# A fused cross-attention and gated feed-forward kernel: K and V of the first group fetched during the K stage, a query unit in two pieces, the last quad in another order

## The reference, cut to what matters

```python
def _L0_xattn_ref(latents, context, Wq, Wk, Wv, Wo):      # latents: layernorm(x); b=8, q_len=128, HIDDEN=512
    hidden_states = jnp.concatenate([context, latents], axis=1)          # 256 keys
    q = (latents @ Wq).reshape(b, q_len, N_KV_HEADS, N_GROUPS, HEAD_DIM) # 4 x 8 heads of 128
    k = (hidden_states @ Wk).reshape(b, kv_len, N_KV_HEADS, HEAD_DIM)
    v = (hidden_states @ Wv).reshape(b, kv_len, N_KV_HEADS, HEAD_DIM)
    scores = jnp.einsum('bqhgd,bkhd->bhgqk', q, k) * scale
    attn = jax.nn.softmax(scores.astype(jnp.float32), axis=-1).astype(q.dtype)
    out = jnp.einsum('bhgqk,bkhd->bqhgd', attn, v)
    return out.reshape(b, q_len, N_HEADS * HEAD_DIM) @ Wo
def _L0_ffn_ref(x, weight, bias, gate_w, in_channel_scale, out_channel_scale):
    routing = jax.nn.softmax((xf @ gate_w.T).astype(jnp.float32), axis=1)   # 8 experts
    in_scale = routing @ in_channel_scale
    out_scale = routing @ out_channel_scale
    wb = ste_sign(weight)                                                   # signs of 512 x 512
    return (xf * in_scale @ wb.T * out_scale + bias)
x = x + _L0_xattn_ref(_layernorm(x), ctx_4096, Wq, Wk, Wv, Wo)
x = x + _L0_ffn_ref(_layernorm(x), weight, bias, gate_w, in_channel_scale, out_channel_scale)
```

## Time and profile before

| what | us |
|---|---|
| median of 3 runs | 686.14 (684.45 to 686.57) |
| the profiled execution | 686.85 |
| its span, first to last instruction | 685.1 |
| outside the span | 1.75 |
| PE busy | 669.3 |
| DVE, ACT, POOL busy | 449.0, 354.3, 301.6 |

### The profile page before, as it was taken

How to read it: one execution, slowest core, us unless ns; L and a number is a source line. 1 busy time by engine, 2 the same in 40 slices (tenths; PEclk the granted TensorE clock), 3 DMA queues, 4 the chain that set the end, 5 groups by cost and what they waited for, 6 DMA issues and landing times.

```text
span 685.1 us, 10290 instructions
## 1 busy us (share of the span) xinstructions
PE 669.3 (98%) x3376; PEld 564.0 (82%) x3376; DVE 449.0 (66%) x752; ACT 354.3 (52%) x881; POOL 301.6 (44%) x248
## 2 busy tenths in 40 slices
PE   7999999999999999999999999999999999989997
PEld 4888887878888888888888888888888888868875
DVE  5653233666767776776677776767767776768766
ACT  3344322744565456545654565556455544566643
POOL 4135000542374337324632463246334638755674
PEclk9999999999999999999999999999999999999999
DMA  9556547688658876766698867667977565645511
GB/s 325 221 206 239 205 203 249 194 262 268 185 190 253 277 244 221 215 186 194 197 279 258 250 190 217 192 191 204 277 271 250 184 203 189 193 152 155 158 42 67
DMA packets 90836, 144.84 MB, mean 211 GB/s; under 512 B 15208, under 2 KB 48232, under 8 KB 89760
## 3 DMA queue, kind: packets, MB, share of 16 engines
q1 hardware_dynamic: 90784, 144.19, 66.1%
HBM read 91.60 MB, written 52.56 MB: 210 GB/s over the span
## 4 chain that ended last, share of the span: by engine, by line
PE 89%; DMA 4%; DVE 3%; ACT 2%; issue 1%; SPq 1%; POOL 0%; ACTq 0%; DVEq 0%
PE bank L1102 48%; PE bank L1216 24%; PE bank L1201 12%; DMA p_park<-p_turned 2%; PE bank L1292 2%; DMA kg<-k_park 1%; DVE bank L920 1%; DMA raw_a<-in_L_xattn_Wv 1%; ACT prob L633 1%; PE bank L1111 1%; PE bank L1243 0%; PE bank L1266 0%; PE bank L1119 0%; POOL p_low L462 0%; ACT wq_pair L550 0%
## 5 line engine op out<-in xcount | busy, mean ns | idle before, releaser
L462 POOL TENSOR_TENSOR p_low<-p_low,p_high 128x1024 fp32r<-128x1024 f32 x64 | 153.6, 2400 | 268.0 <-ACT p_high L550 267.9
L1216 PE MATMUL bank<-wo_pair,oT 128*128 128x512 f32 x768 | 188.3, 392 | 1.5 <-DVE oT L812 1.5
L1102 PE MATMUL bank<-xT,wq_pair 128*128 128x512 f32 x768 | 185.4, 391 | 0.0
L1216 PEld LDWEIGHTS bank<-wo_pair,oT 128*128 128x128 f32 x768 | 139.9, 188 | 28.4 <-issue 2.1
L1102 PEld LDWEIGHTS bank<-xT,wq_pair 128*128 128x128 f32 x768 | 140.5, 188 | 26.7
L633 ACT ACTIVATE prob<-bank,nmax 128x256 f32<-128x256 f32 x256 | 118.9, 470 | 34.3 <-DVE nmax L890 34.2
L550 ACT ACTIVATE oT<-bank 128x512 fp32r<-128x512 f32 x64 | 38.4, 600 | 185.7 <-DVE bank L920 185.5
L905 DVE STREAM_TRANSPOSE p_turned<-prob 128x512 f32<-128x512 f32 x128 | 91.1, 711 | 57.1 <-ACT prob L633 57.1
L1102 PEld LDWEIGHTS bank<-kg,qT 128*128 128x128 f32 x768 | 107.6, 190 | 12.0 <-DMA kg<-k_park 1.9
L1102 PE MATMUL bank<-kg,qT 128*128 128x256 f32 x768 | 111.5, 283 | 2.0 <-DMA kg<-k_park 1.5
L890 DVE TENSOR_REDUCE nmax<-bank 128x2 f32<-128x512 f32 x128 | 87.6, 686 | 37.8 <-PE bank L1102 37.8
(11 more groups left out here) (92 smaller groups left out, 602.3 us busy)
## 6 DMA issues: line engine op xcount, KB each, us to landing
p_park<-p_turned SPq DMA_DIRECT2D x64, 512.0 KB, 4.1
p_low<-p_park SPq DMA_DIRECT2D x64, 512.0 KB, 4.6
r_all<-r_park SPq DMA_DIRECT2D x64, 256.0 KB, 4.4
v_park<-v_stage SPq DMA_DIRECT2D x8, 1024.0 KB, 4.3
raw_a<-in_L_xattn_Wq SPq DMA_DIRECT2D x32, 256.0 KB, 5.2
raw_b<-in_L_xattn_Wo SPq DMA_DIRECT2D x32, 256.0 KB, 4.9
k_park<-k_stage SPq DMA_DIRECT2D x8, 1024.0 KB, 3.8
kg<-k_park SPq DMA_DIRECT2D x32, 256.0 KB, 5.4
```

The lines of the kernel that those rows point to most:

```text
L462: nc.gpsimd.tensor_tensor(part, part.bitcast(fp32), p_high[:, :].rearrange("p i c q -> p (i c q)"), ALU.subtract).then_inc(p_lo, 1)
L1102: last = nc.tensor.matmul(dst, left(a, c), right(b, c), start=(n == 0), stop=(n == 3 * chunks - 1))
L1216: last = nc.tensor.matmul(wo_bank[:, :], oT[:, s, h, :], wo_pair[:, w, h, :], start=((s, w) == TERMS[0] and h == 0), stop=((s, w) == TERMS ...
```

## The change

It does six things. (1) SP loads `kg` and `vg` of the first group in the K stage, right behind the parks of units 2 to 5, four batches at a time; the tiles are laid out anew so that they lie on `wv_pair` and `craw`, which are free by then. (2) At the start, the transposes of the first x come after the whole first product; the second product waits for the high part of x alone at first; DVE makes all four low parts of Wv before the first `layer_norm`, and the second batch's statistics after it. (3) The fourth query unit (u = 3 of the first quad) is made in two pieces, the 128 columns of batch 0 first. (4) In the last quad, ACT's `p_half(t + 1)` comes before `exps(t + 3, 0)`, and in step 1 DVE's statistics of batch 0 come after `o_scale(1)`. (5) In steps 5 and 6 the HI part of `ffn_product(t - 3)` comes before `logits(t - 2)`, and in step 7 there is none: `ffn_product(4)` and its `ffn_scale` are in the tail. (6) In the tail the products, logits and routes stand in another order, and product 5 has a bank of its own.

```diff
@@ -298,6 +302,20 @@
+                if u == 2:
+                    sp.wait_ge(proj_ready, 2 * B)
+                    sp.wait_ge(ct_ready, B)
+                    for i in range(2):
+                        sp.wait_ge(v_parked[i], 16 * (B // 2))
+                if 2 <= u < 2 + NHALF:
...
+                    for b in range(half * HALF, (half + 1) * HALF):
+                        load_k(0, b)
+                elif 4 <= u < 6:
+                    for b in range((u - 4) * HALF, (u - 3) * HALF):
+                        load_v(0, b)
@@ -618,8 +627,14 @@
+                done = 0
+                if first and u == QH - 1:
+                    done = T
+                    nc.scalar.activation(qT[:, HI, h, 0:T], proj_bank[u % 2][:, 0:T], ACT.Copy,
+                                         scale=SCALE).then_inc(first_hi, 1)
+                    act.wait_ge(first_lo, 1)
+                nc.scalar.activation(qT[:, HI, h, half * 512 + done:(half + 1) * 512],
@@ -838,13 +853,12 @@
             for c in range(HC):
-                if c == 2:
-                    dve.wait_ge(x_in[1], 16)
-                    layer_stats(1, 1)
-                    layer_norm(0, 0)
...
+            layer_norm(0, 0)
+            dve.wait_ge(x_in[1], 16)
+            layer_stats(1, 1)
             xt_rest(0)
@@ -1017,8 +1038,11 @@
-                ffn_stats(t - 1)
+                if t > 1:
+                    ffn_stats(t - 1)
                 o_scale(g, qd, t)
+                if t == 1:
+                    ffn_stats(t - 1)
@@ -1136,9 +1161,11 @@
-                            {1: lambda: pe.wait_ge(ct_lo, 1), 2: lambda: xt_transpose(0)}
-                            if n == 0 else {}
+                            {0: {1: lambda: pe.wait_ge(ct_lo, 1)},
+                             1: {1: lambda: pe.wait_ge(xt_lo, 1)}}.get(n, {})
                             ).then_inc(proj_ready, 1)
+                    if n == 0:
+                        xt_transpose(0)
@@ -1174,7 +1201,10 @@
+                if g == 0 and qd == 0 and t == 0 and p == 1:
+                    pe.wait_ge(proj_lo, PRE_UNITS + QH - 1)
+                    pe.wait_ge(first_lo, 1)
@@ -1325,6 +1357,8 @@
                 attend(g, qd, t)
+                if LEAD <= t < B - 1 and t + LEAD >= B:
+                    ffn_product(t - 3, (HI,))
                 if t >= 2:
                     logits(t - 2)
@@ -1333,8 +1367,8 @@
-                if t >= 3:
-                    ffn_product(t - 3)
+                if LEAD <= t < B - 1:
+                    ffn_product(t - 3, (HI, LO) if t + LEAD < B else (LO,))
@@ -1365,14 +1399,15 @@
             logits(B - 2)
-            ffn_product(B - 3, (HI,))
+            ffn_product(B - 4)
             y_transpose(B - 1)
             route_transpose(B - 2)
+            ffn_product(B - 3, (HI,))
+            logits(B - 1)
+            channel_scales(B - 2)
             ffn_product(B - 3, (LO,))
-            channel_scales(B - 2)
-            logits(B - 1)
+            route_transpose(B - 1)
             ffn_product(B - 2, (HI,))
-            route_transpose(B - 1)
             channel_scales(B - 1)
```

More of the change, by code:

```diff
@@ L335, in fetch_r @@
                              ).then_inc(r_in[t % 2], 16)
[L337 to L340, removed]
             park_p(0, 0, 0)
@@ L620, in q_half @@
                     act.wait_ge(s_ready[h // 2], steps(g, qd, HALF * (half + 1) - B))
-                nc.scalar.activation(qT[:, HI, h, half * 512:(half + 1) * 512],
-                                     proj_bank[u % 2][:, :], ACT.Copy, scale=SCALE
+                done = 0
[5 more added lines that the diff above has]
+                nc.scalar.activation(qT[:, HI, h, half * 512 + done:(half + 1) * 512],
+                                     proj_bank[u % 2][:, done:512], ACT.Copy, scale=SCALE
                                      ).then_inc(proj_hi, 1)
@@ L754, in final_step @@
                     gate_exp(t - 2)
+                if t + 1 < B:
+                    p_half(g, qd, t + 1)
                 if t + LEAD < B:
@@ L876, in _, with q_rest @@
                              k_stage[:, u % 2, :, HI, :, kc, :]).then_inc(proj_lo, 1)
-            def q_rest(g, qd, u):
+            def q_rest(g, qd, u, first=False):
                 half, h = divmod(u, QH)
+                done = 0
+                if first and u == QH - 1:
+                    done = T
+                    dve.wait_ge(first_hi, 1)
+                    nc.vector.scalar_tensor_tensor(qT[:, LO, h, 0:T], proj_bank[u % 2][:, 0:T], SCALE,
+                                                   qT[:, HI, h, 0:T], ALU.mult, ALU.subtract
+                                                   ).then_inc(first_lo, 1)
                 dve.wait_ge(proj_hi, count(g, UNITS, qd, PRE_UNITS + u + 1))
-                cols = slice(half * 512, (half + 1) * 512)
-                nc.vector.scalar_tensor_tensor(qT[:, LO, h, cols], proj_bank[u % 2][:, :], SCALE,
+                cols = slice(half * 512 + done, (half + 1) * 512)
+                nc.vector.scalar_tensor_tensor(qT[:, LO, h, cols], proj_bank[u % 2][:, done:512], SCALE,
                                                qT[:, HI, h, cols], ALU.mult, ALU.subtract
@@ L1035, in final_step @@
                     gate_factor(t - 2)
[L1036 removed]
+                if 3 <= t < B - 1:
                     ffn_scale(t - 3)
@@ L1052, in _ @@
             for u in range(QH):
-                q_rest(0, 0, u)
+                q_rest(0, 0, u, first=True)
             for t in range(LEAD):
@@ L1071, in _ @@
             gate_route(B - 2)
+            ffn_scale(B - 4)
             gate_factor(B - 2)
-            ffn_scale(B - 3)
-            z_make(B - 2)
-            gate_max(B - 1)
-            z_rest(B - 2)
-            gate_route(B - 1)
-            gate_factor(B - 1)
+            gate_max(B - 1)
+            z_make(B - 2)
+            gate_route(B - 1)
+            z_rest(B - 2)
+            gate_factor(B - 1)
+            ffn_scale(B - 3)
             z_make(B - 1)
@@ L1285, in ffn_product @@
                             pe.wait_ge(sgnt_copied, HC)
-                        elif b < B - 2:
+                        elif b < B - 3:
                             pe.wait_ge(scaled_ready, b)
+                        elif b == B - 3:
+                            pe.wait_ge(acc_ready, steps(G - 1, QUADS - 1, B))
                         else:
```

29 lines of the change are left out of this document (12 added, 17 removed).

## The result

The changed kernel takes 696.04 us (median of 4 runs, 694.54 to 696.66) beside 685.89 for the kernel before in the same runs: a ratio of 1.0135, 95% interval 1.0117 to 1.0152. By the ratio it is 9.3 us slower (by the medians 10.15), where 684.8 was predicted and the range ended at 687.2. Its profiled execution takes 695.43 us and has a span of 693.6, 8.5 longer than the 685.1 before.

What follows compares the result with a forecast made beforehand. PE, busy 669.3 of 685.1 us, was taken as the bound. Terms 0.3 - 1.5 - 0.2 - 0.1 + 1.7 - 0.3 - 1.5 = -1.6 gave 685.25 from 686.85; it said 684.8, range 682.5 to 687.2.

Steps and rivals of the forecast that it cites:

- steps 1 to 4: Last quad: later statistics lose time, earlier `p_half` wins it back; together -0.1 us (-0.5 to +0.5).
- the tail: Step 7 to the last product: -0.3 us without product 4 before the projection, then -1.5 (+0.2 to -2.0).
- Steps 5 and 6: Last quad: HI parts ahead of the logits make each LO part wait longer, +0.85 us per step, +1.7 in all.
- statistics +1.2: Step 1 of the last quad: statistics after `o_scale(1)` delay `o_half(1)` and PE's projection by 1.2 us.
- `p_half` -1.5: Step 2 of the last quad: POOL finishes before `attend(2)`, so the 1.2 us wait and a smaller one go.
- "just late": Steps 5 and 6: `z_half` arrives slightly late for the HI part, adding 0.15 us before the logits end.
- the order's terms: Tail: product 4 adds 1.84 us, vanishing waits give -2.3, a new wait for the last z adds 0.65.
- The clock term of -1.7: Tail: the 3.7 us stretch at half clock would run at full clock, PE being denser, saving 1.7 us.
- the clock falls in step 7: Rival: the 2.2 us gap brings half clock in the projection behind it, costing 1.7 us, 686.5; chance 0.17.
- The early parts: Before the last quad: start +0.3 us, loads in the K stage -1.5, fourth query unit in pieces -0.2.
- start and query unit: First product's new order +0.3 us (0 to +0.5); fourth query unit in pieces -0.2 (-0.8 to +0.1).
- The rival of parks crowded out: K stage: under 337 GB/s, loads delay parks until ACT waits; +5.1 us at 280 GB/s, 689.9; chance 0.08.

Runs made afterwards that it cites:

- run 8: Changed kernel with `p_half` behind the exps again and products 2 and 3 whole behind the logits again: 687.74 us, ratio 1.0022.
- run 9: Kernel before, with `p_half` ahead of the exps in the last quad and the route's exponentials read from PSUM: 685.45 us, ratio 0.9987.
- run 6: Changed kernel with matmuls nobody reads in PE's gaps, four ahead of each LO part, seven ahead of the last projection: 691.23 us, ratio 1.0065.
- run 10: Kernel before, with only the HI parts of products 2 and 3 moved ahead of the logits: 689.63 us, ratio 1.0047.
- run 3: Kernel before, with only the new start, early loads and query unit in pieces; last quad as before: 685.54 us, ratio 0.9988.
- run 7: Kernel before, with the new tail alone (product 4 moved into the tail, new order on all engines): 686.93 us, ratio 1.0006.
- run 11: Kernel before, with only the `kg` and `vg` loads of the first group in the K stage: 685.25 us, ratio 0.9982.
- run 4: Kernel before, with only `p_half` moved ahead of the exps in the last quad: 688.28 us, ratio 1.0024.
- run 2: Changed kernel with products 2 and 3 whole and behind the logits again: 689.24 us, ratio 1.0035.
- runs 1: Changed kernel with `p_half` behind the exps again in the last quad: 692.05 us, ratio 1.0091.
- run 5: Changed kernel with `gate_route` reading the route's exponentials from a second copy in PSUM: 690.86 us, ratio 1.0067.

## Why the prediction was wrong

It failed in two steps of its sum, steps 1 to 4 and the tail, and mis-sized a third.

- **"Steps 1 to 4: together -0.1 (-0.5 to +0.5)."** This step failed. Its parts were right: statistics +1.2 (measured +1.13 in run 8, with PE's wait for `oT` at 1.82 us where near 1.9 was forecast), `p_half` -1.5 less something (measured -0.29 and -1.05 in run 9). What it left out is the instruction that the move puts in parallel: `p_rest` on POOL moved from behind DVE's route operations onto them, and held one in each of steps 2 to 5. That is +3.0 in steps 2 to 4, and in step 5 a late z, a wait of 0.74 for `z_half` that I had taken as "just late", 0.15, with a late route behind it (run 6). I asked what became ready earlier, not what ran at the same time.
- **"Steps 5 and 6: +1.7."** Right in mechanism and nearly in size: the LO parts wait 1.10 each, the steps grow by 1.05, +2.1 (run 10). The text itself said that the moved matmuls fill no wait but lengthen one; it did not ask what the longer wait does to the clock. That cost 1.6 with this edit alone (run 10), and 2.5 in the two steps of the changed kernel (run 6), so the term came to +6.1 in the two steps instead of +1.7: 3.6 waits, of which 1.5 are the hold's, and 2.5 clock.
- **"Step 7 and the tail: -0.3, and -1.5."** The -0.3 is right (-0.35). Of the tail, the order's terms were right too: with full clock the stretch from projection to last product takes 14.44 us (run 6; 13.6 was forecast) beside 14.45 in the trace of run 3, where the clock is full as well and product 4 lies ahead of the stretch; so waits of some 1.85 went in exchange for the product's 1.84. The clock term of -1.7 is what failed, twice. The half clock before had cost 0.65 (15.11 less 14.45) up to the last product and 0.33 within it (2.48 less 2.15), not 1.7, and the gap in step 7 let the clock fall where the work is dense: +0.9 alone (run 7), +2.85 behind the waits of steps 5 and 6 (17.29 less 14.44). It was the rival "the clock falls in step 7", priced at 1.7 for one stretch and given 0.17; three stretches came, two of them in steps 5 and 6, where the prediction had not looked for any.
- **The early parts** were right in the main, -1.0 for -1.4: `kg` wait gone, loads hidden (-1.3 in run 11 for -1.5), POOL's chain still the end of the first probabilities, start and query unit near nothing. The rival of parks crowded out did not come, with the queue at a mean of 344 GB/s in the stretch shown, above the 337 below which it was to come.

No edit alone accounts for the 9.3 us: alone, on the kernel before, `p_half` costs 1.7 (run 4), the products 3.1 (run 10), the tail 0.6 (run 7), the statistics 1.1 by their rows, and the early parts give 1.0 back (run 3), 5.5 in all, where the intervals of these runs together leave some 2.3 open. The remaining 4 comes only with the edits together. The rows show two parts of it. The clock costs 4.7 more than before in the changed kernel (5.3 by run 6, less the 0.65) and 2.5 in runs 7 and 10 together; and the waits of step 5 are 2.6 together (run 6), where the order alone makes 1.05 (run 10) and `p_half` alone 0.65 (run 4, 9.30 for 8.65). Run 6 shows that the clock is the cause of its part: with the gaps filled and the order unchanged, 4.8 us are gone.

The Trainium skill has the first mechanism, and the prediction should have used it. "SBUF — State Buffer" (section "Who interferes with whom") says that a DVE instruction with two SBUF inputs contends with a GpSimd instruction that reads SBUF, and one in a two-port mode, which `tensor_scalar` can enter, with any: whichever starts first has the shared ports for its whole length and the other stands still. The traces agree: 2.22 to 2.32 us when POOL was first, 0.16 when DVE was first by 0.03 us (617.20 and 617.23), 0.17 with one of the inputs in PSUM. Whether the held `TENSOR_SCALAR` was in such a mode no run shows.

**What stays open.** Which wait lets the clock fall. Gaps of 2.01 us in step 7 were followed by half clock in run 7 and by full clock in run 2, whose clock had fallen in step 1 instead, behind a wait of 1.82 (projection 2.75 us at 612.06). A wait of 1.10 us in step 6 was followed by half clock in the changed kernel, and by full clock in runs 1, 5 and 10. At the end of the kernel, with the old tail, it fell in the traces of before and of runs 4, 9 and 11 and stayed full in those of runs 3 and 10. The runs show that filling the gaps keeps the clock, not which gap would have lost it. Also open is why the last quad begins anywhere from 595.5 to 597.4 in the traces with the early loads.

## What to carry to other kernels

When an instruction is moved earlier, look at what the other engines run beside its new place: here DVE operations of 0.17 us on SBUF alone took up to 2.3 us because POOL's 2.4 us operation on SBUF had started first, and for the one with two inputs reading one of them from PSUM avoided this (run 5). When an edit lengthens a wait of TensorE, give half clock in the dense matmuls behind it a chance and a price of its own (0.9 to 2.85 us for a stretch of the changed kernel, with waits of 1.1 to 2.0 us ahead of them), and test it with matmuls that fill the gap. Edits that each lengthen a wait can cost more together than alone (9.3 beside 5.5 here), so runs of one edit each need not add up.

## What the runs showed of the hardware

- A `TENSOR_TENSOR` of 128x8, 0.17 us by itself, took up to 2.33 us (run 6; 2.32 in the changed kernel) beside a POOL `TENSOR_TENSOR` of 128x1024 and ended within 0.03 us of it; POOL's own took 2.37 to 2.40, no longer than elsewhere.
- Shorter POOL operations hold it too: in step 7 of the changed kernel the route's two operations take 0.74 and 1.19 us and end with POOL's additions to `acc` of 1.27 us each.
- Fifteen useless matmuls, 3.4 us of PE at full clock (15 x 0.227), made the changed kernel 4.8 us faster (run 6).
